# Moving the first value product ahead of the first Q projection in a band attention kernel

## The chip, the cores and the metric

The kernel runs on one core of a Trainium2 chip. The metric is the device time of one execution in microseconds. Before the change it was 1987.71 us, the median of three runs (1987.32 to 1992.75). TensorE (PE) multiplies matrices, VectorE (DVE), ScalarE (ACT) and GpSimd (POOL) work on rows, and SyncE (SP) only issues DMAs. Each engine works through its own list in order and is held back by semaphores alone.

## The reference

For each of 8 batches of 1024 rows and 512 columns the reference computes a layer norm, a banded attention with 16 heads, and a small network for each of 64 columns; both are added to x:

```
xn = _layernorm(x, axis=-1)
Q, K, V = heads of (xn @ Wq + bq), (xn @ Wk + bk), (xn @ Wv + bv)    # 16 heads of 64
scores  = einsum('bhid,bhjd->bhij', Q, K)
columns = where(|i - j| <= 64, scores, 0.0)
attn    = softmax(columns, axis=-1)          # over all 1024 columns, zeros included
out     = (attn @ V).reshape(B, N, 1024) @ Wo + bo
s = xn @ Win + bin_;  h = relu(s[..., None] * W1 + b1)
g = einsum('btmh,mh->btm', h, W2) + b2;  ffn = g @ Wout + bout
result = x + out + ffn
```

Positions outside the band have score 0, not minus infinity, so each row has a constant part (e0) beside its window of 256 columns.

## The kernel before

Every float32 product is made of two float16 parts, high and low, multiplied in three passes (hi*hi, hi*lo, lo*hi). So each operand is split: ScalarE writes the high part, and VectorE or GpSimd the low part as a difference.

The work runs in steps. Step n projects Q, K and V of a pair of heads (pair k = n mod 8 of batch b = n / 8), computes scores and softmax of the pair of step n - 1 (j in the code), and the value product and output product of the pair of step n - 2 (o). There are 66 steps; eight steps are a batch. What a step of TensorE holds, in order: scores(0), scores(1), project_qk(0) (the first half of Q), weigh_values(0), scores(2), scores(3), project_qk(1), weigh_values(1), and then the V projections, project_out(0) to (7) and project_qk(2) and (3). With k = 0, 6 or 7 the transposes of x and the small network's products are added.

The softmax of step n goes round all engines. scores(tp) (L1141) writes two banks for each of four groups of tiles. VectorE's mask_scores(tp) (L884) masks and scales them into probs and gets the row maxima. ScalarE's exps(tp) (L546) takes exponentials and row sums. VectorE's denominators(half) (L896 to L903) makes inv_l and neg_e from two groups. GpSimd's normalise_weights(half) (L401) scales eight tiles of probs; ScalarE's weights_high(half, h) (L604) writes p_hi, and GpSimd's weights_low(half, h) (L416) writes p_lo. SP transposes p_hi and p_lo of each half and head with a DMA (transpose_weights, L246) into pT. weigh_values(half) (L1205) of the next step waits for four of these transposes (pT_in[half]) and for the transposed values (v_got); it is written for the pair whose softmax was made one step earlier. ScalarE's weighted_sums(half) (L612, L616) reads its result, and GpSimd's output_low(half) (L408) makes the low part that project_out needs.

GpSimd's list in a step is output_low(0), normalise_weights(0), weights_low(0, 0), output_low(1), normalise_weights(1), weights_low(0, 1), (1, 0), (1, 1); with k = 0 add_biases stands before normalise_weights(1), with k = 1 two of them stand at the end, and with k = 5 inverse_deviation stands before normalise_weights(1).

SP's list in a step has eight transposes of weights, two of values, and loads of the next step's V, Q and K weights from the kept split copies (load_kept, L225). The load of Q waits until project_qk(2) of the step has read the old ones.

The order on each engine is the order in which the code is written; no scheduler changes it. Some buffers bind the order: probs is overwritten by mask_scores(0) of the next step when weights_low(0, 0) and (0, 1) are done, and by mask_scores(2) when all weights_low are done. PSUM bank 6 is shared by weigh_values(0) and the first V projection, bank 7 by project_qk(0) and project_out(0).

## Time and profile before

| | |
|---|---|
| median of three runs | 1987.71 us |
| the profiled execution's own time | 1987.71 us |
| its span, first to last instruction | 1986.0 us |
| PE, DVE, ACT, POOL busy | 94%, 78%, 76%, 81% |
| granted TensorE clock, mean | 0.983 |
| DMA queue q1 | 277.87 MB, 66.6% of 16 engines' span |

A row of the profile names the source line, the engine, the operation, the tensors written and read (out<-in), and times in microseconds from the span's start. Idle time in brackets is that of the engine just before the row, followed by what ended it. L numbers are lines of the kernel before.

### The profile page before, as it was taken

How to read it: one execution, taken by the hardware profiler on the slowest of the kernel's cores; microseconds unless marked ns; L12 is line 12 of the kernel's file. 1: busy time of each engine (PE TensorE's matmuls, PEld its weight loads, DVE VectorE, ACT ScalarE, POOL GpSimd, SP SyncE). 2: the span in 40 equal slices, each digit the busy share in tenths (PEclk: the TensorE clock that was granted, in tenths of full speed). 3: DMA queues.
4: the chain of work that ended last, by engine and by line, in shares of the span. 5: the costliest groups of instructions: out<-in, count | busy, mean ns of one | idle time of the engine just before them, and what ended most of it. 6: DMA issues, size and time to landing. Idle time of an engine off the chain costs nothing.

```text
span 1986.0 us, 41966 instructions
## 1 busy us (share of the span) xinstructions
PE 1872.8 (94%) x13699; PEld 1024.8 (52%) x13699; DVE 1550.0 (78%) x4195; ACT 1515.4 (76%) x4089; POOL 1603.8 (81%) x2272
## 2 busy tenths in 40 slices
PE   8889989999999999999999999999999999999995
PEld 4444544455555555555555555555555455555543
DVE  6899866887778877788678877788777887688764
ACT  5988866877778777887777887877777787778763
POOL 3778767987788877888779886898868987788885
PEclk8999999999999999999999999999999999999997
DMA  5676546866577666877559766686747866576755
GB/s 158 150 166 147 133 97 138 184 131 134 107 181 164 129 124 115 183 154 134 121 111 197 152 134 118 136 190 132 140 102 160 181 131 124 112 164 134 149 104 131
DMA packets 745593, 280.56 MB, mean 141 GB/s; under 512 B 682504, under 2 KB 694816, under 8 KB 745376
## 3 DMA queue, kind: packets, MB, share of 16 engines
q1 hardware_dynamic: 745328, 277.87, 66.6%
q8 instruction: 110, 1.80, 0.4%
q14 instruction: 107, 0.88, 0.1%
q10 hardware_dynamic: 48, 0.01, 0.0%
HBM read 84.84 MB, written 25.17 MB: 55 GB/s over the span
## 4 chain that ended last, share of the span: by engine, by line
PE 40%; POOL 31%; ACT 11%; issue 8%; DVE 6%; DMA 4%; SPq 1%; POOLq 0%; DVEq 0%; ACTq 0%
PE ps L1155 22%; POOL probs L401 15%; POOL p_lo L416 12%; PE ps L1170 7%; ACT probs L546 5%; PE ps L1205 4%; PE ps L1141 3%; DMA pT_lo<-p_lo 3%; POOL oT_lo L408 2%; POOL acc L423 1%; DVE probs L884 1%; PE ps L1192 1%; PE ps L1180 1%; ACT o_sum L616 1%; PE ps L1081 1%
## 5 line engine op out<-in xcount | busy, mean ns | idle before, releaser
L1155 PE MATMUL ps<-xT_hi,w_split 128*128 128x512 f16 x3072 | 986.3, 383 | 20.3 <-DMA w_split<-w_kept 11.1
L416 POOL TENSOR_TENSOR p_lo<-probs,p_hi 128x256 f16<-128x256 f32 x1024 | 723.3, 706 | 83.7 <-ACT p_hi L604 6.1
L401 POOL TENSOR_SCALAR probs<-probs,inv_l,neg_e 128x256 f32<-128x256 f32 x1024 | 628.3, 629 | 116.1 <-DVE neg_e L903 115.9
L546 ACT ACTIVATE probs<-probs,neg_max 128x256 f32<-128x256 f32 x1024 | 505.9, 499 | 148.4 <-DVE neg_max L891 148.4
L1155 PE MATMUL ps<-xT_lo,w_split 128*128 128x512 f16 x1536 | 586.8, 382 | 0.0
L1155 PEld LDWEIGHTS ps<-xT_hi,w_split 128*128 128x128 f16 x3072 | 301.8, 98 | 396.2 <-issue 24.1
L884 DVE CUSTOM_DVE_ANT_0 probs<-ps,mask,unit_s 128x256 f32<-128x256 f32 x1024 | 433.0, 477 | 64.9 <-PE ps L1141 48.5
L918 DVE SCALAR_TENSOR_TENSOR acc<-ps,unit_o,acc 128x512 f32<-128x512 f32 x512 | 357.3, 739 | 61.4 <-PE ps L1170 61.2
L1170 PE MATMUL ps<-wo_split,oT_hi 128*128 128x512 f16 x1024 | 308.0, 383 | 15.8 <-POOL oT_lo L408 6.7
L604 ACT ACTIVATE p_hi<-probs 128x1024 f16<-128x1024 f32 x256 | 267.8, 1052 | 66.4 <-POOL probs L401 66.3
L408 POOL TENSOR_TENSOR oT_lo<-o_sum,oT_hi 128x512 f16<-128x512 f32 x128 | 152.4, 1190 | 150.8 <-ACT o_sum L616 150.4
L1155 PEld LDWEIGHTS ps<-xT_lo,w_split 128*128 128x128 f16 x1536 | 151.2, 98 | 154.9 <-issue 3.2
L1205 PE MATMUL ps<-pT_hi,v 128*64 128x256 f16 (+1 forms) x2560 | 195.9, 255 | 22.8 <-DMA pT_lo<-p_lo 20.3
L546 ACT ACTIVATION_READ_ACCUMULATOR probs<-probs,neg_max 128x1 f32 x1024 | 196.0, 191 | 0.0
L1170 PE MATMUL ps<-wo_split,oT_lo 128*128 128x512 f16 x512 | 195.4, 382 | 0.0
L1141 PE MATMUL ps<-kT_hi,qT_hi 64*128 64x256 f32 x1024 | 161.4, 311 | 29.6 <-DVE acc L918 15.0
L1205 PEld LDWEIGHTS ps<-pT_hi,v 128*64 128x64 f16 x2560 | 139.6, 111 | 78.6 <-issue 64.7
L1170 PEld LDWEIGHTS ps<-wo_split,oT_hi 128*128 128x128 f16 x1024 | 98.6, 99 | 139.5 <-DVE xT_lo L773 8.7
L1205 PE MATMUL ps<-pT_lo,v 128*64 128x256 f16 (+1 forms) x1280 | 167.3, 253 | 0.0
L960 DVE SCALAR_TENSOR_TENSOR qT_lo<-ps,bias_scaled,qT_hi 128x512 fp32r<-128x512 f32 x128 | 95.2, 744 | 88.3 <-ACT qT_hi L596 88.3
L960 DVE SCALAR_TENSOR_TENSOR kT_lo<-ps,bias_scaled,kT_hi 128x512 fp32r<-128x512 f32 x128 | 95.1, 743 | 78.3 <-ACT kT_hi L596 77.8
L1141 PE MATMUL ps<-kT_lo,qT_hi 64*128 64x256 f32 x1024 | 146.5, 281 | 0.0
(115 smaller groups left out, 2506.8 us busy)
## 6 DMA issues: line engine op xcount, KB each, us to landing
w_split<-w_kept SPq DMA_DIRECT2D x168, 256.0 KB, 3.1
acc<-in_L_attn_x SPq DMA_DIRECT2D x14, 1024.0 KB, 7.4
out_x<-acc SPq DMA_DIRECT2D x14, 1024.0 KB, 5.8
wo_split<-wo_kept SPq DMA_DIRECT2D x56, 256.0 KB, 2.9
w_kept<-w_split SPq DMA_DIRECT2D x24, 256.0 KB, 3.0
pT_hi<-p_hi SPq DMA_TRANSPOSE x256, 3.2
pT_lo<-p_lo SPq DMA_TRANSPOSE x256, 3.3
acc<-in_L_attn_x SPq DMA_DIRECT2D x4, 512.0 KB, 5.8
```

Of the source, the lines that this page charges most:

```text
L401: pool.tensor_scalar(probs[:, h, t], probs[:, h, t], inv_l[:, c:c + 1], neg_e[:, c:c + 1], ALU.mult, ALU.add).then_inc(normed, 1)
L408: pool.tensor_tensor(oT[lo][:, cols], o_sum[half][:], oT[hi][:, cols], ALU.subtract) \
L416: pool.tensor_tensor(p_split[lo][:, h, t], probs[:, h, t], p_split[hi][:, h, t], ALU.subtract).then_inc(p_lo, 1)
L546: act.activation(probs[:, h, t], probs[:, h, t], ACT.Exp, bias=neg_max[:, c:c + 1], accum_out=row_sum[:, c:c + 1])
L604: act.activation(p_split[hi][:, h, tiles], probs[:, h, tiles], ACT.Copy).then_inc(p_hi, 1)
L884: dve.tensor_tensor_reduce(out=probs[:, h, t], in0=ps[SCORE_BANK[tp][h]][:, i * WIN:i * WIN + WIN], in1=mask[:], scale=unit_s[:, j % PAIRS ...
L918: dve.scalar_tensor_tensor(acc[:, parity, t], ps[OUT_BANK[t]][:], unit_o[:, pair % PAIRS:pair % PAIRS + 1], acc[:, parity, t], ALU.mult, A ...
L960: dve.scalar_tensor_tensor(part[lo], ps[QK_BANK[s]][:], bias_scaled[:, Q_ + s % 2, k:k + 1], f32(part[hi]), ALU.add, ALU.subtract).then_in ...
L1141: last = pe.matmul(ps[SCORE_BANK[tp][h]][:, i * WIN:i * WIN + WIN], qT[qp][rows, t * P:t * P + P], kT[kp][rows, t * P:t * P + WIN], start= ...
L1155: last = pe.matmul(dst[:], w[wp][:, i, c], xT[xp][:, c, half * LINE:half * LINE + LINE], start=(c == 0 and a == 0), stop=(c == KC - 1 and ...
L1170: last = pe.matmul(ps[OUT_BANK[t]][:], oT[op][:, t * P:t * P + P], wo[wp][:], start=(a == 0), stop=(a == 2))
L1205: last = pe.matmul(ps[PV_BANK[half]][h * D:h * D + D, q0:q0 + (end - first) * P], v[:, o % 2, vp, (4 * half + c) % T, h], pT[half][h][pp][ ...
```

## The change

Four lists are reordered; no instruction is added, removed or altered.

```diff
@@ SP, step @@
                     transpose_weights(j, 1, 0, hi)
+                    transpose_weights(j, 0, 1, lo)
                 if proj:
                     next_weights(Q_)
-                if attend:
-                    transpose_weights(j, 0, 1, lo)
@@ ACT, step @@
-                if attend:
-                    exps(0)
                 if out_proj:
                     weighted_sums(0)
                 if attend:
+                    exps(0)
                     exps(1)
@@ ACT, step @@
                     values_high()
+                if attend:
+                    weights_high(1, 0)
                 if proj:
                     qk_high(2)
-                if attend:
-                    weights_high(1, 0)
@@ PE, step @@
                     scores(0)
                     scores(1)
-                if proj:
-                    if n == 1:
-                        pe.wait_ge(ffn_s_in, 2 * b + 2)
-                    project_qk(0)
                 if out_proj:
...
                     pe.wait_ge(v_got, 32 * (o + 1))
                     weigh_values(0)
+                if proj:
+                    if n == 1:
+                        pe.wait_ge(ffn_s_in, 2 * b + 2)
+                    project_qk(0)
                 if attend:
                     masks_read(0)
```

The first place is TensorE's list near the start of a step, before. L1141 is scores, L1155 a projection, L1205 weigh_values.

```order
L1141 MATMUL ps<-kT_lo,qT_hi 128x256 x2
L1141 MATMUL ps<-kT_hi,qT_lo 128x256 x2
L1155 MATMUL ps<-xT_hi,w_split 128x512 [waits w_got_q]
L1155 MATMUL ps<-xT_lo,w_split 128x512
L1155 MATMUL ps<-xT_hi,w_split 128x512
L1205 MATMUL ps<-pT_hi,v 64x128 [waits pT_in_0,v_got]
L1205 MATMUL ps<-pT_hi,v 64x128
```

The same place after the change, where the lines of the code are two fewer (L1139, L1153, L1203).

```order
L1139 MATMUL ps<-kT_lo,qT_hi 128x256 x2
L1139 MATMUL ps<-kT_hi,qT_lo 128x256 x2
L1203 MATMUL ps<-pT_hi,v 64x128 [waits pT_in_0,v_got]
L1203 MATMUL ps<-pT_hi,v 64x128
L1203 MATMUL ps<-pT_lo,v 64x128 x2
L1153 MATMUL ps<-xT_hi,w_split 128x512 [waits w_got_q]
L1153 MATMUL ps<-xT_lo,w_split 128x512
```

The value product with its wait for pT_in_0 now stands directly behind scores(1), and the projection behind it.

The second place is ScalarE's list at the start of a step, before. L546 and L549 are exps, L612 and L616 weighted_sums.

```order
L546 ACTIVATE probs,row_sum<-probs,neg_max 128x256 [waits max_ready]
L546 ACTIVATE probs,row_sum<-probs,neg_max 128x256 x3
L549 ACTIVATE e<-neg_max 128x4
L612 ACTIVATE oT_hi<-ps,v_back 128x512 [waits out_done,v_back_ready,pv_done]
L616 ACTIVATE o_sum<-ps,v_back 128x512 [waits oT_lo]
```

After the change, one line number lower:

```order
L611 ACTIVATE oT_hi<-ps,v_back 128x512 [waits out_done,v_back_ready,pv_done]
L615 ACTIVATE o_sum<-ps,v_back 128x512 [waits oT_lo]
L545 ACTIVATE probs,row_sum<-probs,neg_max 128x256 [waits max_ready]
L545 ACTIVATE probs,row_sum<-probs,neg_max 128x256 x3
L548 ACTIVATE e<-neg_max 128x4
```

Both blocks of exps now stand behind the reading of weigh_values(0).

The third place is SP's list in the second half of a step, before.

```order
L246 DMA_TRANSPOSE pT_hi<-p_hi 128x8x128 [waits p_hi,pv_done]
L225 DMA w_split<-w_kept 128x1024 [waits qk_proj]
L246 DMA_TRANSPOSE pT_lo<-p_lo 128x8x128 [waits p_lo,pv_done]
L246 DMA_TRANSPOSE pT_hi<-p_hi 128x8x128 [waits p_hi,pv_done]
L225 DMA w_split<-w_kept 128x1024 [waits qk_proj]
```

After the change:

```order
L246 DMA_TRANSPOSE pT_hi<-p_hi 128x8x128 [waits p_hi,pv_done]
L246 DMA_TRANSPOSE pT_lo<-p_lo 128x8x128 [waits p_lo,pv_done]
L225 DMA w_split<-w_kept 128x1024 [waits qk_proj]
L246 DMA_TRANSPOSE pT_hi<-p_hi 128x8x128 [waits p_hi,pv_done]
L225 DMA w_split<-w_kept 128x1024 [waits qk_proj]
```

The transpose of (half 0, head 1, lo) and the load of the next Q weights have changed places.

## Rows read from the trace of the kernel before

**Rows 1.** Who waited for whom: us in total, times, longest.
```profile
POOL oT_lo L408 <- ACT o_sum L616: 150.4, 58, 11.7
...
PE ps L1205 <- DMA pT_lo<-p_lo: 20.3, 24, 5.4
```

**Rows 2.** Busy time by stretch, batch 4: steps with k = 4 and 7, all eight.
```profile
1111.60:1138.70 27.10, 27.10 (x205) 14.79 (x204) 23.93 (x66) 22.24 (x62) 23.11 (x33) 1.00 0.65 134
...
1197.90:1229.60 31.70, 30.00 (x227) 17.07 (x226) 22.43 (x64) 23.57 (x65) 23.22 (x36) 1.00 0.59 127
sum 236.70, PE 229.72 PEld 125.51 DVE 188.60 ACT 184.30 POOL 197.78; mean PE 28.72 PEld 15.69 DVE 23.58 ACT 23.04 POOL 24.72
```

**Rows 3.** Timeline of PE: weigh_values(0) of steps 32, 36, 37, 38; start of step 36.
```profile
997.19 0.25 PE L1205 MATMUL ps<-pT_hi,v 128*64 128x128 f16 x2
...
1111.56 0.39 PE L1141 MATMUL ps<-kT_hi,qT_hi 64*128 64x256 f32 x2
...
1113.19 0.39 PE L1155 MATMUL ps<-xT_hi,w_split 128*128 128x512 f16 x1
...
1115.88 0.25 PE L1205 MATMUL ps<-pT_hi,v 128*64 128x128 f16 x2
...
1117.32 0.39 PE L1141 MATMUL ps<-kT_hi,qT_hi 64*128 64x256 f32 x2
...
1143.08 0.25 PE L1205 MATMUL ps<-pT_hi,v 128*64 128x128 f16 x2
...
1172.05 0.25 PE L1205 MATMUL ps<-pT_hi,v 128*64 128x128 f16 x2 [0.83 <-DMA pT_lo<-p_lo]
```

**Rows 4.** Timeline of ACT and DVE in step 36: weighted_sums, exps(1), neg_max, denominators.
```profile
1117.56 0.67 ACT L612 ACTIVATE oT_hi<-ps,v_back 128x512 f16<-128x512 f32 x1
...
1118.69 0.50 ACT L546 ACTIVATE probs<-probs,neg_max 128x256 f32<-128x256 f32 x1
...
1120.26 0.17 DVE L891 TENSOR_SCALAR neg_max<-row_max 128x4 f32<-128x4 f32 x1
...
1120.89 0.17 DVE L896 SCALAR_TENSOR_TENSOR row_l<-e,row_sum 128x8 f32<-128x8 f32 x1 [0.46 <-ACT e L549]
```

**Rows 5.** Timeline of POOL: normalise_weights(0) of k = 0, 1, 2, 4.
```profile
1003.01 4.31 POOL L401 TENSOR_SCALAR probs<-probs,inv_l,neg_e 128x256 f32<-128x256 f32 x8 [1.70 <-DVE neg_e L903]
...
1036.35 5.46 POOL L401 TENSOR_SCALAR probs<-probs,inv_l,neg_e 128x256 f32<-128x256 f32 x8 [1.70 <-DVE neg_e L903]
...
1066.41 5.77 POOL L401 TENSOR_SCALAR probs<-probs,inv_l,neg_e 128x256 f32<-128x256 f32 x8
...
1121.81 4.74 POOL L401 TENSOR_SCALAR probs<-probs,inv_l,neg_e 128x256 f32<-128x256 f32 x8 [1.71 <-DVE neg_e L903]
```

**Rows 6.** Timeline of SP: transpose (0, 1, lo) of k = 0, 1, 2, 4.
```profile
1025.90 1.24 SPq L246 DMA_TRANSPOSE pT_lo<-p_lo  x1
...
1053.93 1.24 SPq L246 DMA_TRANSPOSE pT_lo<-p_lo  x1
...
1084.39 1.24 SPq L246 DMA_TRANSPOSE pT_lo<-p_lo  x1
...
1139.76 1.24 SPq L246 DMA_TRANSPOSE pT_lo<-p_lo  x1
```

**Rows 7.** The page: DMA issues, KB each, median us from issue to landing.
```profile
w_split<-w_kept SPq DMA_DIRECT2D x168, 256.0 KB, 3.1
...
pT_lo<-p_lo SPq DMA_TRANSPOSE x256, 3.3
```

**Rows 8.** Batch 0: two waits of PE at step starts, and PE's stretches behind them.
```profile
137.15 0.39 PE L1141 MATMUL ps<-kT_hi,qT_hi 64*128 64x256 f32 x2 [3.21 <-DVE acc L918]
...
169.75 0.58 PE L1141 MATMUL ps<-kT_hi,qT_hi 64*128 64x256 f32 x2 [3.31 <-DVE acc L918]
...
137.00:141.00 4.00, 3.85 (x35) 1.00 0.93 104
...
169.00:173.00 4.00, 3.25 (x26) 0.57 0.75 133
```

## The prediction

> **What bounds the kernel now.** I read the list of who waited for whom first, then the busy time of each engine per step, then one undisturbed step on every engine, and last the transposes' issues. The reader should see in [rows 1] that TensorE waits only 20.3 us in the whole run for the transposed weights (pT_lo) that weigh_values reads, and in [rows 2] that the eight steps of batch 4 take 236.7 us with 229.7 us of TensorE work, so little can be won; the step with k = 4 has no idle TensorE at all (27.1 of 27.1 us). The granted clock stands at 1.00 there, the higher level (2.4 GHz).
>
> A kernel that is full on one engine can still be close to a second limit. I look for it as a loop. Call W the first matmul of weigh_values(0) in a step (L1205). The loop is: W, then scores(2), mask_scores(2) on VectorE, denominators(0), normalise_weights(0) on GpSimd, GpSimd's chain up to the eighth p_lo, the transpose of (half 0, head 1, lo), and W of the next step, which waits for all four transposes of half 0. In the undisturbed step W starts at 1115.88, the GpSimd normalisation at 1121.81, that is 5.9 us later [rows 3, 5]. The transpose is issued at 1139.76, 18.0 us after that [rows 5, 6], and a pT_lo transpose lands a median of 3.3 us after its issue [rows 7]. Sum: 5.9 + 18.0 + 3.3 = 27.2 us. W to W is 1143.08 - 1115.88 = 27.2 us too [rows 3]. So the loop is already as long as TensorE's own work in such a step; W comes at the landing. This is what the change meets.
>
> **The change, part by part.**
>
> TensorE: nothing is added or removed. weigh_values(0) goes ahead of project_qk(0). Before, W stands at the step's start + 4.3 us (1115.88 - 1111.56), behind scores(0), scores(1) and project_qk(0). Now only the two scores are in front: project_qk(0) begins at + 1.6 (1113.19) and takes 2.7 us (to 1115.88) [rows 3]. So W asks for its transposes 2.7 us earlier, at + 1.6. They do not land earlier: SP issues the transpose right when GpSimd has finished, and moving it ahead of the Q weights' load on SP takes nothing away from that wait. What is queued behind W on TensorE is everything, and project_qk(0) no longer fills the wait; it now lies behind W and ahead of scores(2).
>
> The loop's first part gets longer, on two ways that end together:
> - by VectorE: W to scores(2) was 1117.32 - 1115.88 = 1.4 us [rows 3]; now project_qk(0), 2.7 us, is between: 4.1. scores(2) to the start of neg_max after mask_scores(2) is 1120.26 - 1117.32 = 2.9, its row 0.2, and row_l to GpSimd's start is 1121.81 - 1120.89 = 0.9 [rows 3 to 5]. Sum 8.1 us.
> - by ScalarE: weighted_sums(0) starts 1.7 us after W (1117.56) and exps 1.1 us after that (1118.69). One block of exps up to denominators is 1120.89 - 1118.69 = 2.2 us [rows 4]. As exps(0) now stands behind weighted_sums(0), two blocks follow W: 1.7 + 1.1 + 2.1 + 2.2 + 0.9 = 8.0 us.
> So W to normalise_weights(0) is 8.1 us in place of 5.9.
>
> GpSimd's part, from the start of normalise_weights(0) to the issue of the transpose: k = 0: 1025.90 - 1003.01 = 22.9 (add_biases is within); k = 1: 1053.93 - 1036.35 = 17.6; k = 2: 1084.39 - 1066.41 = 18.0; k = 4: 18.0 [rows 5, 6]. I take 18.0 for k = 3 and 5 as well. The landing adds 3.3, and W follows at once; with 0.1 for the semaphore this part is 3.4 us.
>
> W to W, after: from k = 0, 8.1 + 22.9 + 3.4 = 34.4 us. From k = 1, 8.1 + 17.6 + 3.4 = 29.1. From k = 2 GpSimd itself is late, since add_biases closes step 1: normalise to normalise was 1066.41 - 1036.35 = 30.1 us [rows 5], so W(3) comes 8.1 + 30.1 + 18.0 + 3.4 = 59.6 us after W(1). From k = 3, 4 and 5, 8.1 + 18.0 + 3.4 = 29.5 each. Together W(0) to W(6): 34.4 + 59.6 + 88.5 = 182.5 us. Before it was 1172.05 - 997.19 = 174.9 [rows 3]. That is + 7.6 us a batch. Steps 6 and 7 carry the small network's matmuls, so TensorE's own work (30.0 us in a step 7 of 31.7 [rows 2]) is longer than the 29.5 us loop; there TensorE catches up. In these exps(1) comes somewhat earlier (8.1 us after a W at + 1.6 is + 9.7, against 1121.81 - 1111.56 = + 10.2), worth at most 0.4 us where TensorE waits for ScalarE's value rows. Net + 7.2 a batch.
>
> Seven batches have this pattern: 50 us. Batch 1 begins with a long first step and its first loop is not the limit (- 1), and in the last batch step 5 has no inverse_deviation (- 1 to - 2). I take 47. In batch 0 the weights are split as well and TensorE waits about 3.3 us at step starts for VectorE [rows 8]; this is another limit, a step is longer than the new loop, and I count 0 there, bounded by 5 us either way.
>
> The other edits. (a) The Q weights' load on SP now stands behind the transpose, 1.3 us later than it (its issue takes SP 1.24 us [rows 6]); it lands 3.1 us after its issue [rows 7], 4.4 us after the transpose's issue. project_qk(0) is wanted 3.4 + 1.4 = 4.8 us after it. Hidden behind weigh_values(0); 0 us, and if the load meets other traffic up to 1 us a step, 35 us over the 35 steps concerned. (b) weights_high(1, 0) ahead of qk_high(2): ScalarE now waits there for four of GpSimd's normalisations, with qk_high(2), its low part and add_output(4), (5) behind, for which the next scores(0) waits. I count 0, since the next W is later than this; below nothing is not excluded, as p_hi comes up to one ScalarE row sooner, but GpSimd reaches those rows last. Both ends stay within 1 us a batch. (c) GpSimd's output_low(0) has its operand earlier; it waited 150.4 us for it in all [rows 1], but behind it GpSimd waits for denominators(0) anyway, so this is worth nothing.
>
> The clock. Before W of step 3 TensorE now stands idle for 59.6 - 29.1 - 27.2 = 3.3 us. In the first batch two such waits, 3.21 and 3.31 us, were followed by a granted clock of 1.00 and of 0.57 in the next 4 us [rows 8]: one of two such waits brought the lower level (1.2 GHz). 4 us at 0.57 cost 1.7 us, and they fall on weigh_values(0) and project_qk(0), inside the loop. The wait of step 3 is as long as the one that did, so I take 0.7 x 1.7 x 7 = 8 us; ends: 0, and 1.7 us for each of the 35 long waits, 60.
> The Trainium skill says in "TensorE: Matmul & The Clock Gate", section "HAM oscillation — how this bites in real kernels", that DMA waits between bursts of matmuls make the clock fall back each time, so that every burst starts cold. By that rule all 35 waits would cost, which is the third rival below; by the row with 1.00 none would. The trace of before agrees in one of its two rows.
>
> Sum: 47 + 0 + 8 = 55 us on the profiled execution's 1987.7 us (span 1986.0 and 1.7 around it, and equal to the median of the three): 2043 us.
>
> **Rivals.**
> 1. Faster. If the transposes of half 0 land before + 1.6, W never waits, the step keeps its order of work and the 20.3 us of [rows 1] go: 1967 us. It is decided by the landing of the lo transpose: before + 1.6 or after. For it: GpSimd idles before its output and normalisation rows, and in steps 6 and 7 there is room. Against: in the undisturbed step it lands at about 1143.0, + 4.3 in the next step. 6%.
> 2. No change: the new wait takes the place of TensorE's other waits. A batch has 236.7 - 229.7 = 7.0 us of them [rows 2], and 1.7 us of that lie in step 7. If the remaining 5 us gave way to the wait for W, + 7.2 would be + 2; with GpSimd's rows 0.5 us shorter per step, 0: 1988 us. Against: the 7.2 already compares W with W, so those waits are in it. 5%.
> 3. The clock falls after each wait for W: 47 + 60 = 107 us, 2095 us. For: [rows 8] once of twice. Against: most of the waits for W would be 2 us, not 3.3. 9%.
> 4. The forecast: the loop through W binds in steps 1 to 5. 80%.
>
> **How the numbers follow.** The likeliest case gives 2043. Its size: 0.5 us more or less in the 8.1 us, over 35 loops, is 17 us; clock 0 to 25; (a) up to 15. So 2018 to 2078 for the case itself. That leaves out nearly all of rivals 1 to 3, about 20%, and stays the range. About 0.3% (6 us) is what a measurement of this kernel can tell from no change. Faster 0.06, same 0.05, slower 0.89.
>
> **What would show it.** TensorE's wait for pT_lo at weigh_values should grow from 20.3 us to about 70 to 90 us, with some 2 us in each of steps 1 to 6 of a batch, about 3 in step 3, and none in step 7. W to the GpSimd normalisation should read 8.1 us, and the part from there to the transpose's issue remain at 17.6 to 18.0. Steps 1 to 5 should take 29 to 30.5 us, step 7 stay near 31.7. TensorE's busy time should stay within 1%. If the wait of W stays near 20 us, or W to normalise remains at 5.9 us, the forecast is wrong. If PEclk shows 9 or less in many slices and the time is over 2080, rival 3 was right. If TensorE waits for w_split<-w_kept in each step, term (a) was mis-sized.

## The result and the profile after the change

The changed kernel takes 2048.88 us (median of 4 runs, 2041.57 to 2050.58), the kernel before 1988.45 us on the same chip (4 runs, 1987.32 to 1992.75). The ratio is 1.0292, with a 95% interval of 1.0263 to 1.0322: slower by about 60 us. The forecast was 2043 us.

The profiled execution took 2055.2 us, its span is 2053.5 us, 67.5 us more than before. First the waits of TensorE and GpSimd in the whole span: who waited, on which line, for what; then us, times, and the longest.

```profile
PE ps L1203 <- DMA pT_lo<-p_lo: 95.3, 48, 6.4
...
PE ps L1139 <- DVE acc L916: 20.1, 12, 3.2
...
PE ps L1153 <- DMA w_split<-w_kept: 0.9, 3, 0.5
...
POOL probs L400 <- DVE neg_e L901: 250.6, 64, 16.0
...
POOL oT_lo L407 <- ACT o_sum L615: 83.3, 43, 4.9
```

In the kernel before, the row for neg_e was:

```profile
POOL probs L401 <- DVE neg_e L903: 115.9, 61, 15.6
```

The wait for pT_lo at weigh_values grew from 20.3 us [rows 1] to 95.3. GpSimd's wait for its output operand shrank by 67 us, from 150.4 to 83.3, and its wait one instruction later, in front of normalise_weights for neg_e, grew by 135 us, from 115.9 to 250.6: the earlier operand bought nothing. The head of the page shows the same.

```profile
PE 1889.2 (92%) x13699; PEld 1038.7 (51%) x13699; DVE 1533.6 (75%) x4195; ACT 1511.1 (74%) x4089; POOL 1603.0 (78%) x2272
...
PEclk8989999999999999999999999999999999999997
...
POOL 48%; PE 25%; issue 14%; ACT 6%; DMA 3%; DVE 3%; POOLq 0%; DVEq 0%; ACTq 0%; SPq 0%
```

With the same 13699 matmuls TensorE is busy 1889.2 us, 16.4 us more than the 1872.8 us of before, at a mean granted clock of 0.971 in place of 0.983. The last line gives the shares of the chain that ended last; GpSimd has become its largest part, 48% against 31% before, and TensorE has 25% against 40%.

Batch 4 by step (k = 0 to 7), as in [rows 2]: the window, its length, busy time (instructions) of PE, PEld, DVE, ACT and POOL, granted clock, DMA share, GB/s.

```profile
1027.10:1060.40 33.30, 32.54 (x237) 18.08 (x236) 24.65 (x64) 25.17 (x67) 22.94 (x33) 1.00 0.51 96
1060.40:1088.90 28.50, 27.32 (x207) 14.89 (x206) 21.87 (x61) 22.90 (x63) 23.41 (x34) 1.00 0.74 167
1088.90:1119.00 30.10, 27.25 (x205) 14.80 (x204) 23.96 (x62) 22.85 (x63) 28.36 (x37) 1.00 0.90 193
1119.00:1150.10 31.10, 28.86 (x204) 15.93 (x204) 24.00 (x65) 22.60 (x62) 24.59 (x35) 0.95 0.65 153
1150.10:1179.20 29.10, 27.25 (x207) 14.87 (x206) 24.26 (x66) 22.20 (x62) 24.08 (x35) 1.00 0.62 128
1179.20:1208.30 29.10, 27.25 (x205) 14.80 (x204) 21.85 (x70) 20.91 (x59) 24.08 (x35) 1.00 0.72 128
1208.30:1242.70 34.40, 31.52 (x225) 17.21 (x224) 23.04 (x65) 23.45 (x63) 26.86 (x42) 0.95 0.61 115
1242.70:1273.90 31.20, 30.01 (x229) 17.06 (x228) 22.26 (x64) 23.48 (x65) 23.48 (x36) 1.00 0.63 133
sum 246.80, PE 232.00 PEld 127.65 DVE 185.88 ACT 183.58 POOL 197.79; mean PE 29.00 PEld 15.96 DVE 23.23 ACT 22.95 POOL 24.72
```

The step with k = 4 had 27.1 us, all of it work [rows 2]; it has 29.1 now, with 27.25 us of work. Steps 3 and 6 show a clock of 0.95; step 3 has 1.6 us more "work" than step 4, and step 6 has 1.0 us more than it had before (30.55). The eight steps take 246.8 us in place of 236.7.

The loop in step 36 (k = 4), on TensorE, answering [rows 3]; the first two rows are of step 35. Brackets are the idle time before a row and what ended it.

```profile
1119.02 0.39 PE L1139 MATMUL ps<-kT_hi,qT_hi 64*128 64x256 f32 x2 [1.31 <-DVE acc L916]
...
1122.94 0.25 PE L1203 MATMUL ps<-pT_hi,v 128*64 128x128 f16 x2 [2.22 <-DMA pT_lo<-p_lo]
...
1150.11 0.39 PE L1139 MATMUL ps<-kT_hi,qT_hi 64*128 64x256 f32 x2
...
1153.64 0.25 PE L1203 MATMUL ps<-pT_hi,v 128*64 128x128 f16 x2 [1.85 <-DMA pT_lo<-p_lo]
...
1182.55 0.25 PE L1203 MATMUL ps<-pT_hi,v 128*64 128x128 f16 x2 [1.68 <-DMA pT_lo<-p_lo]
...
1212.88 0.32 PE L1203 MATMUL ps<-pT_hi,v 128*64 128x128 f16 x2 [2.88 <-DMA pT_lo<-p_lo]
```

On the other engines, as in [rows 4 to 6]:

```profile
1155.19 0.69 ACT L611 ACTIVATE oT_hi<-ps,v_back 128x512 f16<-128x512 f32 x1 [4.88 <-PE ps L1203]
...
1156.35 0.51 ACT L545 ACTIVATE probs<-probs,neg_max 128x256 f32<-128x256 f32 x1
...
1160.73 0.16 DVE L894 SCALAR_TENSOR_TENSOR row_l<-e,row_sum 128x8 f32<-128x8 f32 x1
...
1161.63 4.76 POOL L400 TENSOR_SCALAR probs<-probs,inv_l,neg_e 128x256 f32<-128x256 f32 x8 [3.79 <-DVE neg_e L901]
...
1179.37 1.23 SPq L246 DMA_TRANSPOSE pT_lo<-p_lo  x1
```

W (the first row of weigh_values(0)) to GpSimd's normalisation: 1161.63 - 1153.64 = 8.0 us (5.9 before). Normalisation to the transpose's issue: 17.7. Issue to the next W: 3.2. W to W: 28.9 us, against 27.2 us of work: TensorE waits 1.7 to 1.9 us in such a step (k = 4 and 5), and the wait is the loop's excess.

Step 35 (k = 3) waits twice: 1.31 us in front of scores(0) for an addition to acc, and 2.22 us in front of W. Step 38 (k = 6) waits 2.88 us; the steps of k = 6 in batches 2, 3, 5 and 6 wait 2.4.

Over the span, from before to after: batch 0 222.4 to 230.4 us; batch 1 249.9 to 254.7 (its first step, number 8, shrank by 7.3 us, from 46.1 to 38.8, and the rest grew by 12.1); batches 2 to 7 together 1420.2 to 1474.7, some 9 us each.

### The profile page after: what moved, and what is told of

Same layout as the page of the kernel before. It is cut to its first block, busy times and chain, and to the rows that moved or that the text cites. A ratio compares the mean times of both kernels' runs of the same rounds, so it can differ in the third digit from the quotient of the medians.

```text
span 2053.5 us, 41966 instructions
## 1 busy us (share of the span) xinstructions
PE 1889.2 (92%) x13699; PEld 1038.7 (51%) x13699; DVE 1533.6 (75%) x4195; ACT 1511.1 (74%) x4089; POOL 1603.0 (78%) x2272
## 4 chain that ended last, share of the span: by engine, by line
POOL 48%; PE 25%; issue 14%; ACT 6%; DMA 3%; DVE 3%; POOLq 0%; DVEq 0%; ACTq 0%; SPq 0%
POOL probs L400 22%; POOL p_lo L415 20%; PE ps L1153 12%; PE ps L1203 4%; PE ps L1168 4%; DMA pT_lo<-p_lo 3%; POOL oT_lo L407 3%; POOL acc L422 3%; PE ps L1139 2%; ACT probs L545 2%; PE ps L1190 1%; ACT o_sum L615 1%; PE ps L1079 1%; ACT oT_hi L611 1%; DVE probs L882 1%
## 5 line engine op out<-in xcount | busy, mean ns | idle before, releaser
L1153 PE MATMUL ps<-xT_hi,w_split 128*128 128x512 f16 x3072 | 992.4, 385 | 10.0 <-issue 4.5
L400 POOL TENSOR_SCALAR probs<-probs,inv_l,neg_e 128x256 f32<-128x256 f32 x1024 | 614.9, 617 | 250.6 <-DVE neg_e L901 250.6
L415 POOL TENSOR_TENSOR p_lo<-probs,p_hi 128x256 f16<-128x256 f32 x1024 | 734.9, 718 | 81.9 <-ACT p_hi L603 2.9
L1153 PE MATMUL ps<-xT_lo,w_split 128*128 128x512 f16 x1536 | 589.9, 384 | 0.0
L545 ACT ACTIVATE probs<-probs,neg_max 128x256 f32<-128x256 f32 x1024 | 505.4, 499 | 13.9 <-DVE neg_max L889 13.9
L1153 PEld LDWEIGHTS ps<-xT_hi,w_split 128*128 128x128 f16 x3072 | 303.4, 99 | 387.6 <-issue 34.5
L1203 PE MATMUL ps<-pT_hi,v 128*64 128x256 f16 (+1 forms) x2560 | 210.9, 267 | 95.3 <-DMA pT_lo<-p_lo 95.3
L611 ACT ACTIVATE oT_hi<-ps,v_back 128x512 f16<-128x512 f32 x128 | 86.9, 679 | 247.2 <-PE ps L1203 247.2
L1153 PEld LDWEIGHTS ps<-xT_lo,w_split 128*128 128x128 f16 x1536 | 151.8, 99 | 156.6 <-issue 6.3
L407 POOL TENSOR_TENSOR oT_lo<-o_sum,oT_hi 128x512 f16<-128x512 f32 x128 | 153.0, 1196 | 84.0 <-ACT o_sum L615 83.3
L1203 PEld LDWEIGHTS ps<-pT_hi,v 128*64 128x64 f16 x2560 | 149.5, 116 | 133.2 <-issue 108.9
L1139 PE MATMUL ps<-kT_hi,qT_hi 64*128 64x256 f32 x1024 | 159.3, 307 | 26.7 <-DVE acc L916 20.1
L1203 PE MATMUL ps<-pT_lo,v 128*64 128x256 f16 (+1 forms) x1280 | 176.9, 265 | 0.0
L1139 PE MATMUL ps<-kT_lo,qT_hi 64*128 64x256 f32 x1024 | 145.7, 281 | 0.0
```

Of the source, the lines that this page charges most:

```text
L400: pool.tensor_scalar(probs[:, h, t], probs[:, h, t], inv_l[:, c:c + 1], neg_e[:, c:c + 1], ALU.mult, ALU.add).then_inc(normed, 1)
L407: pool.tensor_tensor(oT[lo][:, cols], o_sum[half][:], oT[hi][:, cols], ALU.subtract) \
L415: pool.tensor_tensor(p_split[lo][:, h, t], probs[:, h, t], p_split[hi][:, h, t], ALU.subtract).then_inc(p_lo, 1)
L545: act.activation(probs[:, h, t], probs[:, h, t], ACT.Exp, bias=neg_max[:, c:c + 1], accum_out=row_sum[:, c:c + 1])
L611: act.activation(oT[hi][:, cols], src[:], ACT.Identity, bias=v_back[:, o % 2:o % 2 + 1], scale=1.0 / P_SCALE).then_inc(oT_hi, 1)
L1139: last = pe.matmul(ps[SCORE_BANK[tp][h]][:, i * WIN:i * WIN + WIN], qT[qp][rows, t * P:t * P + P], kT[kp][rows, t * P:t * P + WIN], start= ...
```

## The experiments

**One edit at a time.** Two accounts stood against each other: TensorE's reordering alone makes the loop and so the loss, or ScalarE's (rival A). The diffs in this section are shortened: a condition and its body stand on one line, and unchanged lines are left out. Each kernel was profiled in one execution.

TensorE's reordering alone (e1_pe):

```diff
                     scores(1)
-                if proj: ... project_qk(0)
                 if out_proj: ... weigh_values(0)
+                if proj: ... project_qk(0)
```

> Only TensorE's edit: weigh_values(0) ahead of project_qk(0); ScalarE keeps exps(0) ahead of weighted_sums(0), SP and the rest as before. Theory (a loop from W, the start of weigh_values(0), to W of the next step): VectorE's way alone, with project_qk(0) between W and scores(2), gives 8.1 us from W to normalise_weights(0), so the loop is about 29 us in steps 1 to 5 and the time is as with the whole change, 2035 to 2052 us, with W waiting 80 to 100 us in all. Rival A (ScalarE's order is the cause, since exps(0) is held back until W is done): this kernel stays within 6 us of the 1988 us before.

Measured: 2092.9 us, ratio 1.050 (1.0463 to 1.0536). Rival A fell: with ScalarE's list as before the wait for pT_lo is there. But the size was missed, by 41 us or more. Its waits of TensorE at weigh_values:

```profile
PE ps L1205 <- DMA pT_lo<-p_lo: 107.4, 50, 5.2
```

Step 36 (k = 4), with the columns of the windows above, and step 51 (k = 3), one that kept the full clock:

```profile
1164.06:1194.92 30.86, 28.86 (x206) 15.32 (x206) 24.26 (x66) 22.54 (x62) 24.28 (x35) 0.94 0.59 120
...
1636.37:1665.68 29.31, 27.23 (x206) 14.86 (x206) 23.36 (x65) 23.22 (x63) 24.23 (x35) 1.00 0.80 162
```

And TensorE in step 36, from W to scores(2):

```profile
1167.75 0.25 PE L1205 MATMUL ps<-pT_hi,v 128*64 128x128 f16 x2 [2.00 <-DMA pT_lo<-p_lo]
...
1169.43 0.61 PE L1155 MATMUL ps<-xT_hi,w_split 128*128 128x512 f16 x1
...
1173.52 0.39 PE L1141 MATMUL ps<-kT_hi,qT_hi 64*128 64x256 f32 x2
```

W of step 52, behind the step at full clock:

```profile
1669.52 0.25 PE L1205 MATMUL ps<-pT_hi,v 128*64 128x128 f16 x2 [2.15 <-DMA pT_lo<-p_lo]
```

Step 36 takes 30.9 us at a mean clock of 0.94, and so does step 37. The wait for W here is 2.00 us, and a projection row behind it lasts 0.61 us; at the full clock the same row lasts 0.39 (shown with e9_kept_busy below). So W to scores(2) is 1173.52 - 1167.75 = 5.8 us instead of the 4.1 of the forecast: the lower clock falls on the loop itself, which grows by 1.7 us. It does not make the next wait longer, since the slowed matmuls lengthen TensorE's own work by as much: step 51 had a clock of 1.00, and the wait of step 52 behind it was 2.15 us, as long as those behind slowed steps (2.0 to 2.1). The wait of 2 us is there in each of these steps, and the clock falls beside nearly each of them. This kernel spends 175 us at the lower clock, before 71, after the whole change 120 (sums of the trace's clock records; up to 2 us of each lie behind the last instruction).

ScalarE's swap of exps(0) and weighted_sums(0) alone (e2_act):

```diff
-                if attend: exps(0)
                 if out_proj: weighted_sums(0)
-                if attend: exps(1)
+                if attend: exps(0); exps(1)
```

> Only ScalarE's edit of weighted_sums(0) ahead of exps(0); TensorE's order as before. Theory: ScalarE's way alone gives 8.0 us from W to normalise_weights(0) (two blocks of exps behind the reading of weigh_values(0)), VectorE's way stays at 5.9; the loop is again 29.4 us and the time 2023 to 2047 us. TensorE's waits are then for pT_lo at W, with W at 5 to 6 us in the step. Rival B (only TensorE's order matters, ScalarE's swap is absorbed): within 6 us of 1988 us.

Measured: 2104.57 us, ratio 1.0535 (1.0479 to 1.0591), worse than expected. W to the normalisation is 7.9 us, as expected. But project_qk(0) still stands ahead of W, so W starts at + 4.3 us in steps 0, 1 and 7 and at 5 to 9 us in steps 2 to 6. TensorE hardly waits there (25.2 us for pT_lo in all); it waits in front of scores(1) for kT_lo and in front of the small network's products for vT (31.0 us, before 13.9). ScalarE has its part in the operands of both, behind weighted_sums(0) and exps in its list. The largest new wait:

```profile
PE ps L1140 <- DVE kT_lo L959: 42.3, 37, 5.8
```

The expectation had counted the loop alone and not ScalarE's later rows. The whole change, where W goes ahead too, has 6.6 us of waits for kT_lo and 10.1 for vT.

SP's order alone, the transpose ahead of the Q load (e3_sp):

```diff
                     transpose_weights(j, 1, 0, hi)
+                    transpose_weights(j, 0, 1, lo)
                 if proj: next_weights(Q_)
-                if attend: transpose_weights(j, 0, 1, lo)
```

> Only SP's edit: transpose (half 0, head 1, lo) ahead of the load of the next Q weights. Theory: no landing that TensorE waits for comes earlier, since the transpose waits for GpSimd; the Q weights come 3 us later, and project_qk(0) here stands ahead of W at + 1.6 us, so it would wait for them at up to 2 us in steps 1 to 5: 0 to + 40 us, with a wait of TensorE for w_split<-w_kept in place of pT_lo. Rival C (the SP edit is harmless in either order): within 4 us of 1988.

Measured: 2170.31 us, ratio 1.0884 (1.0848 to 1.0920), far outside what was expected. The wait of TensorE in the whole span:

```profile
PE ps L1154 <- DMA w_split<-w_kept: 149.5, 43, 5.0
```

and the first projection of step 36, which begins at 1205.11:

```profile
1210.51 0.61 PE L1154 MATMUL ps<-xT_hi,w_split 128*128 128x512 f16 x1 [3.71 <-DMA w_split<-w_kept]
```

SP waits for the p_lo of (half 0, head 1) before it may issue the Q load, and project_qk(0), which in this kernel stands ahead of W, wants the weights at + 1.6 and gets them at + 5.4. The order on SP was costed at nothing in the forecast because project_qk(0) stands behind W there; this run shows that the two edits need each other, and that the price without the other is 176 us (2170.31 against 1994.05 of the kernel before on that chip).

ScalarE's weights_high(1, 0) ahead of qk_high(2) alone (e4_high):

```diff
-                if proj: qk_high(2)
                 if attend: weights_high(1, 0)
+                if proj: qk_high(2)
```

> Only ScalarE's second edit: weights_high(1, 0) ahead of qk_high(2). Theory: qk_high(2), its low part and add_output(4) and (5) come 1 to 1.7 us later, scores(0) of the next step needs them at + 27.2 us and has about 1 us to spare, except in step 2 where GpSimd is 3 us late: 0 to + 10 us in all, TensorE's wait for acc at scores growing. Rival D (p_hi earlier helps GpSimd): - 3 us or better.

Measured: 1985.88 us, ratio 0.9965 (0.9948 to 0.9982). The steady batches stay as long as they were (237.7 us on average, 237.1 before); TensorE's wait for kT_lo (14.5 us before) is 6.7 us and that for acc 28.6 (15.0). What is gained lies in batch 1, whose first step (number 8) goes from 46.1 to 41.1 us. That this edit gains it is not shown: step 8 is shorter than 46.1 us in each of the twelve experiments, also in those without the edit (40.5 us in e1_pe, 43.6 in e3_sp, 42.1 in e10_bias). What shortens it by 7.3 us in the changed kernel stays open.

**Two parts.** TensorE's and ScalarE's order together, without the other two edits (e5_pe_act; the first two diffs above). Rival E held that together they give what the whole change gives, 2045 to 2056.

> TensorE's edit and ScalarE's swap of weighted_sums(0) and exps(0) together; SP and weights_high(1, 0) as before. The loop theory gives W to normalise_weights(0) 8.0 us as in the whole change, so without the clock the same time as that. What differs is the form of TensorE's idle time: in the whole change qk_high(2) comes late and a part of the wait lies at scores(0), in two pieces. Theory now: one wait of 2.1 us or more in a step is followed by a lower granted clock, which keeps itself up, as with TensorE's edit alone (steps of 30.9 us, 175 us at the lower clock): 2070 to 2095 us. Rival E: ScalarE's swap is what makes the whole change quicker than TensorE's edit alone (2049 against 2093): 2045 to 2056 us.

Measured: 2082.46 us, ratio 1.0485 (1.0462 to 1.0508). The expected time held and rival E fell: the SP and weights_high edits, of which the first alone cost 176 us and the second gained 7, take back 34 us here. The expectation's lower clock that "keeps itself up" is not borne out: in this kernel too the waits behind steps at full clock are 2.0 us long (steps 29 and 37), as those behind slowed ones. The reason can be seen in step 36 of both. GpSimd and SP in this kernel:

```profile
1170.79 4.77 POOL L401 TENSOR_SCALAR probs<-probs,inv_l,neg_e 128x256 f32<-128x256 f32 x8 [3.67 <-DVE neg_e L902]
...
1180.51 5.24 POOL L401 TENSOR_SCALAR probs<-probs,inv_l,neg_e 128x256 f32<-128x256 f32 x8
...
1188.71 1.24 SPq L246 DMA_TRANSPOSE pT_lo<-p_lo  x1
...
1192.03 0.24 PE L1204 MATMUL ps<-pT_hi,v 128*64 128x128 f16 x1
```

and in the changed kernel:

```profile
1171.35 4.73 POOL L400 TENSOR_SCALAR probs<-probs,inv_l,neg_e 128x256 f32<-128x256 f32 x8
```

Normalisation to issue is 17.9 us here and 17.7 with all four edits (GpSimd's eight rows of half 1 take 5.24 and 4.73 us), and issue to W 3.3 and 3.2. That is 0.3 us a loop. It makes the wait for W of step 37 2.0 us instead of 1.7, and the clock falls there (0.94): 164 us at the lower level against 120 in the whole span. A third of a microsecond in the loop cost 1.7 us more in a step in which the clock fell too (30.9 us against 29.1 in step 37).

**Other places for the pieces.** project_qk(0) behind scores(2) and (3), with the other lists as before (e6_scores_first). If W to scores(2) is what makes the loop long, this should bring the time back; rival F, that something else waits then, gave 2035 or more.

```diff
                 if out_proj: ... weigh_values(0)
                 ... scores(2); scores(3)
+                if proj: ... project_qk(0)
```

> As TensorE's edit alone, but project_qk(0) goes behind scores(2) and scores(3), so that nothing stands between weigh_values(0) and the scores; the other engines as before. Theory: W to normalise_weights(0) is again about 5.9 us and at least 9.3 us from the step's start (VectorE's four blocks), so two steps take at least 9.3 + 17.7 + 3.1 + 25.5 us, 27.8 us a step; with GpSimd's late step 2 unchanged this is 1988 to 2015 us. Rival F (what costs is that weigh_values(0) waits early at all, whatever follows it): 2035 us or more.

Measured: 2052.38 us, ratio 1.0328 (1.0309 to 1.0346): the expectation missed by 37 us, and the time is that of rival F. scores(2) now comes 2.7 us sooner in the step, and in the code it waits for the last of project_out's results to be added (add_output(7)), so it is held by the additions to acc: by 1.9 us in step 20. W to normalise_weights(0) came to 6.4 to 8.4 us in the steps of k = 4 and 5, not to 5.9. So this run does not settle what the loop would cost with a short way from W to the scores. The wait for pT_lo is shorter than in e1_pe, but a second one came:

```profile
PE ps L1205 <- DMA pT_lo<-p_lo: 74.6, 51, 6.2
...
PE ps L1141 <- DVE acc L918: 61.7, 50, 3.2
```

The changed kernel with weights_low(0, 1) ahead of normalise_weights(1) on GpSimd, so that the lo transpose of half 0 can go some 5 us earlier (e7_low_early; against the kernel after):

```diff
                     output_low(1)
+                    weights_low(0, 1)
                     normalise_weights(1)
-                    weights_low(0, 1)
                     weights_low(1, 0)
```

> The whole change, and on GpSimd weights_low(0, 1) goes ahead of normalise_weights(1), which makes the fourth p_lo pair of half 0 ready 5 us earlier. Theory: W's wait for pT_lo goes (below 30 us in all, from 95.3); the normalisation of half 1 is 2.9 us later, weights_high(1, 0) and (1, 1) on ScalarE with it, and behind them qk_high(2) and (3), so that a wait of about 1 us for kT_lo at scores(1) and for acc at scores(0) comes in its place: 1998 to 2028 us. Rival G (the landing at W is a symptom, GpSimd's total work is the limit, 24 us and more a step): no change from the whole change, 2045 to 2055 us.

Measured: 2113.21 us, ratio 1.0634 (1.0617 to 1.0651), 85 us above what was expected. Its waits:

```profile
PE ps L1204 <- DMA pT_lo<-p_lo: 8.4, 2, 5.7
...
PE ps L1140 <- DVE acc L917: 120.1, 46, 5.6
...
ACT p_hi L604 <- POOL probs L400: 243.3, 99, 6.9
```

The loop through W was broken, as foreseen, and the wait went from 95.3 to 8.4 us. A longer one took its place: half 1 is normalised later, weights_high(1, 0) blocks ScalarE, qk_high(2) and add_output(4), (5) are behind it, and scores(0) waits. The forecast had named this queue in its step (b) and costed it at nothing; that holds only as long as GpSimd's order stays.

The same with SP and ScalarE put in the matching order (e8_low_matched; SP issues the lo transpose of (0, 1) and the Q load ahead of the hi one of (1, 0), ScalarE does qk_high(2) and (3) ahead of the weights_high whose operands are late):

```diff
 SP:   transpose(0, 1, lo); next_weights(Q_); transpose(1, 0, hi); transpose(1, 1, hi)
 ACT:  qk_high(2); weights_high(1, 0); ... qk_high(3); weights_high(1, 1)      (k = 1 to 6)
```

> As the kernel before this one in the list, with two lists matched to it: on SP the transpose (half 0, head 1, lo) and the load of Q come ahead of the transpose (half 1, head 0, hi); on ScalarE qk_high(2) is again ahead of weights_high(1, 0) and qk_high(3) is ahead of weights_high(1, 1) in steps 1 to 6. Theory: neither W nor the scores wait in steps 1, 4 and 5, which take 27.2 to 27.6 us; step 7 keeps its 31.2 us; only step 2, where GpSimd is late by add_biases, still waits: 1968 to 1990 us. Rival G: 2035 us or more.

Measured: 2050.59 us, ratio 1.032 (1.0302 to 1.0337); missed by 60 us or more, at a time that rival G allowed. The matching took back 63 us of the run before, but the wait for kT_lo stands now:

```profile
PE ps L1142 <- DVE kT_lo L961: 65.2, 37, 8.4
```

Steps with k = 2 and 4 came to 28.2 and 28.0 us, those with k = 1 and 3 took 32.9 and 31.0. Which rows ahead of kT_lo's make it late in these two was not followed up, so rival G's reason, GpSimd's total work, is neither shown nor excluded.

**What the clock is worth.** The changed kernel with twelve transposes of the identity, written to a bank of PSUM that weigh_values(0) overwrites, right before W in the steps k = 2 to 6 (e9_kept_busy). They do no part of the computation; they only fill the wait.

```diff
+                    if proj and 2 <= k <= 6:
+                        pe.wait_ge(v_in, 2 * n)
+                        for i in range(12):
+                            pe.transpose(ps[PV_BANK[0]][:, 0:P], ident[:], ident[:])
                     pe.wait_ge(v_got, 32 * (o + 1))
                     weigh_values(0)
```

> The whole change, and in steps 2 to 6 TensorE does 12 transposes of the identity matrix into PSUM bank 6, which weigh_values(0) then overwrites, in the time in which it waits for pT_lo (0.11 us each by the x transposes, 1.3 us together, less than the wait of 1.7 us and more). Theory: the waits of 2.2 us and more in steps 3, 5 and 6 are no longer followed by the lower clock, the time at the lower clock falls from 120 us to 60 to 85 us, and the clock's part of the loss comes back: 2030 to 2044 us. Rival H (the lower clock costs nothing here, since TensorE waits anyway): the clock share rises and the time stays at 2045 to 2055 us.

Measured: 2032.55 us (2030.10 to 2032.81), ratio 1.021 (1.0181 to 1.024), as expected. TensorE in step 36, which begins at 1131.88:

```profile
1133.51 1.53 PE L1239 MATMUL ps<-ident 128*128 128x128 f32 x12
1135.30 0.25 PE L1203 MATMUL ps<-pT_hi,v 128*64 128x128 f16 x2 [0.26 <-DMA pT_lo<-p_lo]
...
1136.74 0.39 PE L1153 MATMUL ps<-xT_hi,w_split 128*128 128x512 f16 x1
```

Steps 35 and 36 by window:

```profile
1102.43:1131.88 29.45, 28.69 (x216) 16.16 (x216) 23.98 (x65) 22.49 (x62) 24.55 (x35) 1.00 0.76 162
1131.88:1160.83 28.95, 28.69 (x217) 16.14 (x216) 24.30 (x66) 22.20 (x62) 24.07 (x35) 1.00 0.64 128
```

W is still at + 3.4, and the step still 28.95 us: the loop is untouched. But the step with k = 3 goes from 31.1 to 29.45 us with a clock of 1.00. In batches 1 to 7 the changed kernel had 13 waits with a lower clock beside them; here no step of batches 2 to 7 has one. The time at the lower clock falls from 120 to 61 us and the kernel gains 2048.88 - 2032.55 = 16 us between the medians. Between the two profiled executions it is 22.7 us, since the changed kernel's was 6.3 us above its median. So of the 60 us about 16 are the clock's, and 44 are left to the loop and batch 0.

**Towards a faster kernel.** GpSimd's bias additions stand inside the loop in step 0 and close step 1 [rows 5]. Moved (e10_bias, against the kernel before): four at the end of the batch before, four in step 0, none in step 1.

```diff
-                if k == 0 and proj: add_biases(0); add_biases(1)
+                if k == 0 and proj and b > 0: add_rows(b, tiles_of(1))
-                if k == 1 and proj and b > 0: add_biases(2); add_biases(3)
+                if k == 7 and proj and not last: add_rows(b + 1, tiles_of(0))
```

> The kernel before, with GpSimd's eight bias additions of a batch moved: four to the end of step 7 of the batch before, four to step 0, none at the end of step 1. Theory: normalise_weights(0) of step 2 comes at + 10.2 us in place of + 13, the transposes of step 2 land 3 us earlier, and the waits of steps 2 and 3 (28.8 and 29.4 us against 27.3 of work) go: 2 to 3.5 us a batch, 1968 to 1978 us. Rival I (these waits are the load of the Q weights and kT_lo, which do not hang on the bias additions): 1984 to 1992 us.

Measured: 1976.17 us, ratio 0.9924 (0.9894 to 0.9954). The mean step with k = 3 goes from 29.4 to 27.8 us. What is gone there is a wait of 1.1 us for kT_lo in front of scores(1), which each of these steps had, and W comes earlier in the step (+ 4.6 us in place of 5.9). The step with k = 2 stays (28.8 and 28.6 us): it waits for the Q weights, as rival I held. With the weights_high edit added (e11_bias_high):

> The kernel before, with the bias additions moved and weights_high(1, 0) ahead of qk_high(2), which alone gave a ratio of 0.9965 and, in steady batches, moved 1.5 us of waiting from step 3 to step 2. Theory: without GpSimd's late step 2 the edit costs nothing there and keeps its gain of about 5 us in batch 1: 1962 to 1976 us, not over the kernel with the moved additions alone.

Measured: 1970.63 us, ratio 0.9898 (0.9864 to 0.9932); the interval overlaps that of e10_bias, so the gain of 5.5 us over it is likely, not certain. Last, the change's order of TensorE and ScalarE only where the network's matmuls leave room in the loop, in steps with k = 0 and 7 (e12_ends):

```diff
+                for part in (first_values, first_queries) if k in (0, 7) else (first_queries, first_values):
+                    part()
```

(ScalarE's list has the same condition around exps(0).)

> As the kernel before this one in the list, and in steps with k = 0 and 7 the order of the change (weigh_values(0) ahead of project_qk(0), weighted_sums(0) ahead of exps(0)), where the transposes land before + 1.6 us; in all others the order before. Theory: W waits nowhere longer, step 7 takes 31.2 us in place of 31.7, normalise_weights(0) of step 0 is 0.5 us earlier: 3 to 5 us less than the kernel without it, 1958 to 1972 us. Rival J: the mixture makes a step follow that is late at its start, no gain or a loss.

Measured: 1961.52 us (1956.90 to 1963.12), ratio 0.9852 (0.9826 to 0.9878): faster than both kernels, and each of its five runs is below the four of e11_bias_high (1968.16 to 1972.50). The gain over that kernel is 9 us where 3 to 5 had been expected. Part of it is the clock: three of the five steps of k = 7 in batches 2 to 6 of e11_bias_high took 33.4 us at 0.95, and all five take 31.2 us at 1.00 here. The earlier normalise_weights(0) in step 0, which the expectation counted, did not come. The wait at weigh_values:

```profile
PE ps L1214 <- DMA pT_lo<-p_lo: 16.7, 14, 6.3
```

and steps 35 and 36 (k = 3 and 4):

```profile
1067.19:1094.92 27.73, 27.23 (x205) 14.81 (x204) 24.20 (x65) 22.81 (x63) 24.08 (x35) 1.00 0.75 171
1094.92:1122.75 27.83, 27.23 (x205) 14.83 (x205) 24.26 (x66) 22.42 (x62) 24.27 (x35) 1.00 0.66 134
```

Without the loop's excess TensorE has 0.5 to 0.6 us of idle time in such a step.

## Why the prediction was right, point by point

- **The loop, + 47 us.** Right in mechanism, and in size to 6 us. W to normalisation 8.0 us (8.1 forecast), GpSimd's part 17.7 (17.6 to 18.0; with k = 5 it is 18.5, where 18.0 had been taken), issue to W 3.2 (3.4), W to W 28.9 (29.5); W(0) to W(6) of batch 4 184.2 us (182.5), in which the lower clock of step 3 lies, not counted there. The two ways of the forecast were also measured one by one: VectorE's alone gives 8.0 us in the steps at full clock of e1_pe, ScalarE's alone 7.9 in e2_act. Before the change the 5.9 us ran by ScalarE, as the wait of 0.46 us for e in [rows 4] shows; after it, row_l follows neg_max without a wait, so VectorE's way ends last. With the clock kept up (e9_kept_busy) the batches 2 to 6 take 244.1 us on average, before 237.1: + 7.0, where + 7.2 was forecast. Over the span that run leaves 44 us; 3 of these are in batch 0 (225.6 us against 222.4), so 41 stand against the 47. The missing 6 are in batch 1, where step 8 became 7.3 us shorter (6.4 in e9_kept_busy) and 1 had been taken. TensorE's order alone brings the wait (e1_pe).
- **Which steps.** No wait in step 7, and waits in steps 1 to 6, as named, but not evenly. In batches 2 to 6 it was 1.2 us in step 1, 1.6 to 2.0 in step 2, 2.2 to 2.6 in step 3, about 1.7 in steps 4 and 5 with two of 2.3, and 2.4 to 2.9 in step 6. The 3.3 us forecast before W of step 3 came in two pieces, 1.31 us at scores(0) and 2.22 at W in batch 4, 3.5 us together. The first is for the additions to acc, the queue that step (b) named. Steps 1 to 5 took 28.4, 30.3, 30.8, 29.0 and 29.5 us on average, for 29 to 30.5; step 7 took 31.2.
- **The wait for pT_lo:** 95.3 us, above the 70 to 90 named.
- **(a) The Q load hidden:** right, 0.9 us of waits; before they had been 11.1 us, a gain not counted. But it is hidden only by the order of TensorE; e3_sp gives 149.5 us without it.
- **(b) weights_high first, 0:** within its bound of 1 us a batch either way when alone (e4_high, - 0.35%). In company it may help more: with SP's edit 34 us. These two were not run apart from each other on top of e5_pe_act, so their shares are open.
- **(c) output_low earlier, 0:** right, the wait moved to the next instruction.
- **The clock, + 8 us in 0 to 60:** too small, within its bounds: 16 us by the medians with e9_kept_busy. TensorE's busy time in the profiled execution rose by 16.4 us; that the two agree is in part chance, since that execution was 6.3 us above the median. The term that failed is the count of one fall a batch, of step 3 alone. Batches 1 to 7 had 13 falls beside a wait, one to three in each batch, and batch 0 has its own, some 5 of the 16 us. In batches 1 to 7 of the changed kernel 10 of 14 waits of 2.0 to 2.5 us and all 3 longer ones stood beside a lower clock, none of 34 waits of 1 to 2 us did. The rate behind the longer waits was taken as 0.7. Of the four waits of 2.7 to 3.5 us at step starts in batch 0 of the kernel before, the prediction read two (one of two with a fall); the other two, of 2.71 and 3.49 us, have one each, so three of four. What was not seen is that the waits of 2 us, which the third rival's "against" called short, belong with them. In the window of 4 us around a W:

```profile
1121.20:1125.20 4.00, 2.26 (x30) 2.26 (x30) 3.96 (x15) 0.00 (x0) 3.54 (x6) 0.76 1.01 223
1151.50:1155.50 4.00, 2.15 (x38) 1.67 (x35) 3.96 (x15) 0.31 (x1) 3.54 (x6) 1.00 0.96 204
```

  The first holds the 2.22 us wait of step 35, the second the 1.85 us wait of step 36. The length of the wait alone does not decide it: a wait of 2.43 us in step 54 had no fall and those of 2.43 to 2.45 us in steps 22, 30 and 46 had one, and in e11_bias_high four waits of 1.7 us in steps with k = 7 stood beside one. Rival 3, a fall after each wait for W, is wrong for this kernel, and nearly right for e1_pe (26 of 30 waits of 2 us or more; 2092.9 us against the 2095 that it gave).
  The Trainium skill's "TensorE: Matmul & The Clock Gate", section "HAM oscillation — how this bites in real kernels", describes a kernel in which waits for DMAs of some 3 to 5 us between bursts bring the clock down each time. The waits here are shorter than those, so the prediction took the section further than it goes when it laid all 35 waits under it. These runs show falls beside most waits of 2 to 3 us, and none beside the shorter ones of the changed kernel.
- **Batch 0, 0 ± 5:** wrong by its size, + 8.1 us. With the wait filled (e9_kept_busy) it is + 3.2, so some 5 of it go with the clock; the other 3 were not pursued.
- **Rivals 1 and 2** fell with the wait: from batch 1 on the transposes of half 0 land after + 1.6 in every step of k = 1 to 6 but one, step 9, the first loop of batch 1, which the forecast had left out.
- **The range.** The three ends named for it, 17 us for the loop, 17 more for the clock and 15 for (a), would reach 2092 us and not 2078; the measured time lies within either.

The sum came close partly because errors offset each other: 6 us too much for the loop of seven batches (41 for 47), 3 too little for the clock there (11 for 8), 8 too little for batch 0. 55 - 6 + 3 + 8 = 60, in round numbers, as medians and single traces are mixed in it. That these offset is luck; the loop's + 7 us a batch is not.

## What to carry to other kernels

Before an instruction that waits is moved ahead of one that does not, add up the loop that it closes through the other engines, from its start in one step to its start in the next; here a loop of 27.2 us under 27.2 us of TensorE work looked like no wait at all, and 2.2 us added to it came back as time in six steps of eight. Parts of a reordering across several queues cannot be priced one by one: alone the four cost + 5.0%, + 5.4%, + 8.8% and - 0.35%, together + 2.9%. What did pay was to take work out of GpSimd's part of the loop (the bias additions, - 0.8%), and to use the new order only in the steps where another limit leaves it room.

## What the runs showed of the hardware

- The granted clock answered to small differences in a repeated wait: with waits of 1.7 us steps of 28.9 us at 1.00, with waits of 2.0 to 2.1 us steps of 30.9 us at 0.94, over several steps in a row in e1_pe. The slowed rows did not make the next wait longer: it was 2.15 us behind a step at 1.00 and 2.0 to 2.1 behind steps at 0.94.
- Twelve transposes (1.53 us of TensorE work with no use) in front of the wait in five steps of eight made the kernel 16 us faster than leaving TensorE idle. None of the 13 falls of the clock beside waits in batches 1 to 7 was left.
- The same eight GpSimd rows (128x256 f32) took 5.24 us in one order and 4.73 in another, while nothing of theirs had changed. What the other engines did beside them differs between the two orders; which of it matters was not tested.
